# Second graph-attention layer: the projection h in twenty 128-column pieces, copied one pair later, and each head's sums normalised one pair earlier

## What is computed

```python
def gat_conv(x, src, dst, W, att_src, att_dst, bias, heads, out_ch):
    h = (x @ W).reshape(N, heads, out_ch)
    a_src = jnp.einsum('nhc,hc->nh', h, att_src)
    a_dst = jnp.einsum('nhc,hc->nh', h, att_dst)
    e = jax.nn.leaky_relu(a_src[src] + a_dst[dst], NEG_SLOPE)
    m = jax.ops.segment_max(e, dst, num_segments=N)
    ex = jnp.exp(e - m[dst])
    s = jax.ops.segment_sum(ex, dst, num_segments=N)
    alpha = ex / (s[dst] + 1e-16)
    out = jax.ops.segment_sum(h[src] * alpha[:, :, None], dst, num_segments=N)
    return out.reshape(N, heads * out_ch) + bias
```

## Time and profile before

| | us |
|---|---|
| median of three runs | 1220.93 |
| lowest and highest run | 1220.03 and 1222.17 |
| the profiled execution, its span | 1220.4 |
| in it: the 64 pairs of this layer, first sum to last `columns` | 909.4 to 1127.2 |

### The profile page before, as it was taken

The page is one execution under the profiler, slowest core; times in us unless marked ns, Lnnn a source line. Parts: engine busy times, 40 slices in busy tenths (PEclk is TensorE's granted clock), DMA queues, the critical chain, the costliest instruction groups (busy, mean ns, idle before and its releaser), DMA issues. The chain is left out here.

```text
span 1220.4 us, 17917 instructions
## 1 busy us (share of the span) xinstructions
PE 1052.0 (86%) x5617; PEld 744.6 (61%) x5622; DVE 778.0 (64%) x1724; ACT 524.2 (43%) x752; POOL 625.3 (51%) x503
## 2 busy tenths in 40 slices
PE   3999899989599999999298799888898888777897
PEld 1454577778477777777055488787773434433575
DVE  6988578628233333332495889996368777787855
ACT  2234544231111111111133478889537776766323
POOL 1000458302557555543410587999478777685242
PEclk9999899855599999999589799999989999989899
DMA  3000003044388999992510111211012111172551
GB/s 117 1 0 1 1 1 137 2 170 151 132 285 296 301 302 307 303 306 94 182 35 1 37 45 43 87 53 36 9 39 69 36 53 35 37 242 72 179 173 42
DMA packets 107987, 134.57 MB, mean 110 GB/s; under 512 B 30240, under 2 KB 76040, under 8 KB 107792
## 3 DMA queue, kind: packets, MB, share of 16 engines
q1 hardware_dynamic: 92720, 112.68, 28.4%
q0 software_dynamic: 15200, 21.04, 5.3%
HBM read 135.03 MB, written 27.45 MB: 133 GB/s over the span
## 5 line engine op out<-in xcount | busy, mean ns | idle before, releaser
L2347 POOL TENSOR_TENSOR am<-CT,qb 128x1024 f32<-128x1024 f32 x128 | 302.2, 2385 | 29.5 <-ACT PT L2376 17.4
L2369 ACT ACTIVATE PS<-adb,ab 128x1024 f32<-128x1024 f32 x128 | 143.1, 1118 | 89.4 <-DVE am L2474 88.2
L2474 DVE TENSOR_TENSOR am<-PS,am 128x1024 f32<-128x1024 f32 x128 | 156.4, 1222 | 37.3 <-ACT PS L2369 30.2
L2468 DVE CUSTOM_DVE_ANT_0 masked<-PS,mask 128x1024 f32<-128x1024 f32 x128 | 156.2, 1220 | 32.4 <-issue 30.6
L2580 PE MATMUL PS<-PT,h 128*65 128x512 f32 x256 | 122.8, 611 | 36.6 <-ACT PT L2376 25.1
L1232 DVE COPY yo<-PS 128x512 f32<-128x512 f32 x64 | 44.3, 691 | 168.5 <-PE PS L1170 163.1
L2567 PE MATMUL PS<-h,PT 128*128 128x129 f32 x1024 | 128.0, 283 | 22.0 <-ACT PT L2376 12.2
L2376 ACT ACTIVATE PT<-am,as 128x1024 f32<-128x1024 f32 x128 | 145.2, 1134 | 0.3 <-DVE am L2474 0.3
L2567 PEld LDWEIGHTS PS<-h,PT 128*128 128x128 f32 x1024 | 121.1, 196 | 30.5 <-issue 18.2
L1197 ACT ACTIVATE hT<-PS,b1T 128x128 f32<-128x128 f32 x128 | 40.0, 363 | 214.8 <-PE PS L1162 195.7
L1162 PE MATMUL PS<-xgT,w1r 128*128 128x128 f32 x1024 | 125.8, 276 | 0.0
(11 more groups left out here) (426 smaller groups left out, 1777.9 us busy)
## 6 DMA issues: line engine op xcount, KB each, us to landing
w2r<-in_L_ffn_W SPq DMA_DIRECT2D x64, 512.0 KB
w1r<-in_L_ffn_W SPq DMA_DIRECT2D x64, 512.0 KB
adb<-a_scratch SPq DMA_DIRECT2D x16, 512.0 KB, 4.0
qb<-q_scratch SPq DMA_DIRECT2D x14, 512.0 KB, 3.8
wc<-in_L_gnn_W SPq DMA_DIRECT2D x4, 1024.0 KB, 9.2
w1x<-in_L_ffn_W SPq DMA_DIRECT2D x2, 2048.0 KB, 11.0
w2x<-in_L_ffn_W SPq DMA_DIRECT2D x2, 2048.0 KB, 9.3
w1x<-in_L_ffn_W SPq DMA_DIRECT2D x7, 512.0 KB, 5.4
```

The source lines that it names most:

```text
L2347: pool.tensor_tensor(am[:, k % RING, :], CT[:, s, :], qb[:, hd % 2, :], ALU.add).then_inc(s_sum, 1)
L2369: act.activation(RELU, adb[:, hd % 2, :], ACT.Relu, bias=ab[:, s, hd:hd + 1]).then_inc(s_relu, 1)
L2468: dve.tensor_tensor_reduce(masked[:], wide(row_bank(hd)), mask[:, t, :], 1.0, -3.0e38, ALU.subtract, ALU.max, mrow[:, hd % 2, t:t + 1]).th ...
L2474: dve.tensor_tensor(am[:, k % RING, :], RELU, am[:, k % RING, :], ALU.add).then_inc(s_all, 1)
```

## The change

The ten units in the loop become twenty pieces of one tile by 128 columns: four for tiles 6 and 7 of heads 0 to 3, and sixteen for heads 4 to 7. `H_AT` puts them behind (0,1), (0,3), (0,5), (0,7), (1,4), (1,6), and in heads 2 to 5 behind s = 0, 4 and 6, in heads 3 and 4 behind s = 7 as well. ACT's copy comes LATE = 1 pair later. `normed` moves from behind the sum of the fifth pair (s = 4) to behind that of the fourth (s = 3). The counts for which `columns` and the weight load wait follow: SP issues the second half of W2 after 10 units, the last of which is now behind (0,7). The first attention layer keeps its numbers.

```diff
--- before.py
+++ after.py
@@ -2196,17 +2196,22 @@
             FQ = FH // 2
             quarters = [[(t + n, 1, slice(q * FQ, (q + 1) * FQ), slice(n * FQ, (n + 1) * FQ)) for n in range(2)]
                         for q in range(2) for t in range(0, NT, 2)]
+            UP_FRONT = 6
             if final:
-                UNITS = [[(t, 0, slice(0, FH), slice(0, FH))] for t in range(NT)] + quarters
-                H0 = 6
-                H_AT = (0, 1), (0, 3), (1, 1), (1, 5), (2, 1), (2, 5), (3, 5), (4, 1), (4, 5), (5, 1)
+                UNITS = [[(t, 0, slice(0, FH), slice(0, FH))] for t in range(UP_FRONT)]
+                for half, tiles in ((0, range(UP_FRONT, NT)), (1, range(NT))):
+                    UNITS += [[(t, half, slice(q * FQ, (q + 1) * FQ), slice(0, FQ))] for q in range(2) for t in tiles]
+                H0 = UP_FRONT
+                FIRST_HALF = UP_FRONT + 2 * (NT - UP_FRONT)
+                H_AT = ((0, 1), (0, 3), (0, 5), (0, 7), (1, 4), (1, 6),
+                        *((hd, s) for hd in range(2, 6) for s in (0, 4, 6, 7) if s < 7 or hd in (3, 4)))
             else:
                 UNITS = [[(NT - 1, 0, slice(0, FH), slice(0, FH))], [(NT - 1, 1, slice(0, FQ), slice(0, FQ))],
                          *([(t, 2, slice(0, FQ), out) for t, _, _, out in unit] for unit in quarters[NT // 2:])]
                 H0 = 3
                 H_AT = (0, 1), (0, 5), (1, 1)
             H_AFTER = dict(zip(H_AT, range(H0, len(UNITS))))
-            LATE = 3 if final else 2
+            LATE = 1 if final else 2
             H_MOVED = {(hd + (s + LATE) // NT, (s + LATE) % NT): i for (hd, s), i in H_AFTER.items()}
             assert H0 + len(H_AT) == len(UNITS)
 
@@ -2217,8 +2222,8 @@
                         return 2 if s == NT - 1 else 0
                     return 2 + s // 2 + 1
                 if hd < HEADS // 2:
-                    return s + 1
-                return NT + (hd - HEADS // 2) // 2 * (NT // 2) + s // 2 + 1
+                    return s + 1 if s < UP_FRONT else UP_FRONT + hd // 2 * (NT - UP_FRONT) + s - UP_FRONT + 1
+                return FIRST_HALF + (hd - HEADS // 2) // 2 * NT + s + 1
 
 
 
@@ -2289,7 +2294,7 @@
                             sp.dma_start(W2t[0][:], W2_d[:, :, 0:HEADS * CH2 // 2]).then_inc(s_w2[0], 16)
                         if final and hd == 1:
 
-                            sp.wait_ge(s_h, NT)
+                            sp.wait_ge(s_h, FIRST_HALF)
                             sp.dma_start(W2t[1][:], W2_d[:, :, HEADS * CH2 // 2:]).then_inc(s_w2[1], 16)
                         if final and hd == HEADS - 2:
                             tail.load_early(sp, len(UNITS))
@@ -2507,7 +2512,7 @@
                     for k in range(PAIRS):
                         hd, s = k // NT, k % NT
                         counted(k)
-                        if hd and s == (4 if final else 1):
+                        if hd and s == (3 if final else 1):
                             normed(hd - 1)
                         for ahead, t in maxima(hd, s):
                             maxed(ahead, t)
@@ -2645,7 +2650,7 @@
                         if (hd, s) in H_AFTER:
                             wait(pe, s_hm, H_AFTER[hd, s])
                             if final:
-                                if H_AFTER[hd, s] == NT:
+                                if H_AFTER[hd, s] == FIRST_HALF:
                                     pe.wait_ge(s_w2[1], 16)
                                 wait(pe, s_ev, hd if s > 2 else hd - 1)
                             else:
```

## The result

| | before | after |
|---|---|---|
| median, us | 1220.48 (4 runs) | 1236.07 (4 runs) |
| lowest to highest | 1219.96 to 1222.17 | 1234.18 to 1237.68 |
| span of the profiled execution | 1220.4 | 1235.8 |
| first sum of the loop to its last `columns` | 217.8 | 236.6 |

The changed kernel is slower by a factor of 1.012 (95% interval 1.0097 to 1.0144), 15.6 us between the medians, where 17.3 were forecast.

The account below looks back on a forecast made before the run. DVE and ACT were taken to set the pace, PE mattering only where one waits for it. +0.4 - 8.7 - 12.5 + 16.3 + 14.8 + 1.6 + 5.4 = +17.3 gave 1238.2 us on the median, range 1230.5 to 1244.0.

Parts of the forecast that it names:

- The waits that go: DVE's late maximum behind (hd,7), heads 1 to 4, -8.7 us; its wait for transposes, heads 1, 2, 4 and 5, -12.5.
- The normalising: Slot behind (hd,3), heads 1 to 5: DVE waits 2.41 us for transposes, slot 5.74 instead of 2.48; +16.3 us.
- The copies: With LATE = 1 ACT waits 1.46 us for a piece, making the next ReLU 1.2 late; +14.8 us together.
- One sign: A sign to look for in the profile: slots of 3.7 us behind s = 7 and about 3.7 behind s = 1.
- The clock: PE idle 3.84 us behind (hd,3) lowers its clock; columns of (hd,4) 1.34 longer in four heads of five, +5.4 us.
- after 3.06 us: Idle stretch of PE in the profile before, after which columns took 1.90 us as always.
- The rival that the clock holds: No fall of PE's clock after the new idle stretch: 1238.2 - 5.4 = 1232.8 us; chance 0.20.
- The one that it stays down over the next piece as well: Piece behind (hd,4) and next columns at half speed, head 2's offsets late: 5 x 3.1, +2, about 1250 us; chance 0.09.
- Heads 6 and 7: No pieces there; only the wait of the earlier normalising counts: +0.4 and +1.2, together +1.6 us.
- Off the path: Second half of W2 about 10 us later, head 2's offsets queue behind it: cost 0, bound 3 us.
- That PE is ahead of the copies: Faster rival: pieces ready when ACT comes, so the copies' +14.8 us go: 1218.0 us; chance 0.05.
- That the delays overlap: No-difference rival: a late ReLU before (hd,3) is taken up by DVE's wait for the transposes; 1222 us; chance 0.04.

Follow-up runs that it names:

- both_back: Changed kernel with LATE = 2 and the normalising behind s = 4 again, only the pieces and their places kept: 1209.47 us, 0.9870 of the kernel before.
- both_w2_later: both_back with SP issuing the second half of W2 behind the write of head 2's offsets: 1199.35 us, 0.9829 of the kernel before.
- norm_after_max: Changed kernel with the normalising still in the slot of (hd,3), but behind that slot's maximum: 1233.11 us, 1.0112 of the kernel before.
- norm_back: Changed kernel with only the normalising put back behind s = 4; pieces and LATE = 1 stay: 1219.45 us, 0.9953 of the kernel before.
- late_two: Changed kernel with LATE = 2, the normalising staying behind s = 3: 1227.19 us, 1.0018 of the kernel before.
- second profile of the change: The changed kernel run again, unaltered, on another chip: 1241.02 us, 1.0177 of the kernel before.
- the two tests with zeros: Changed kernel with ten matmuls of zeros behind columns of (hd,3), heads 1 to 5, run twice: 1234.48 us (1.0074 of the kernel before) and 1231.87 us (1.0093).
- last experiment: both_w2_later with eight maxima of head 7 moved from behind s = 0 and 1 to behind s = 5 and 6: 1199.75 us, 0.9824 of the kernel before.
- pe_kept_busy: Changed kernel with ten matmuls of zeros on PE behind columns of (hd,3) in heads 1 to 5, first run: 1234.48 us, 1.0074 of the kernel before.
- units_behind_six: Kernel before, with its four big units behind (hd,5) of heads 1 to 4 put behind (hd,6): 1220.86 us, 0.9993 of the kernel before.

## Why the prediction came out right, point by point

**The waits that go.** The slots behind (hd,7) of heads 1 to 4 are 2.54, which is 2.11 less than before where 2.17 were counted, and no maximum waits there. In the slots behind (hd,4), 2.47, the wait of 3.1 is gone. That the two are real gains, and not hidden by something else, is shown by both_back and both_w2_later: with the pieces alone the kernel gains 1.3% and 1.7%, 15.5 and 20.7 us, where 21.2 were taken off. Of the 5.7 that the first lacks, the late offsets are 3.4.

**The normalising.** 5.74 was worked out, and five slots of 5.74 or 5.75 were measured. That the wait is for the transposes was shown by norm_after_max, and that it costs 16.3 and more by norm_back.

**The copies.** Worked out were 1.46 us of waiting, 0.13 in which the copy holds ACT and a ReLU 1.2 late; the rows show 1.3 to 1.4 in most places where the clock held, 0.16, and slots of 3.68 and 3.65 (2.48 + 1.2). The late_two kernel takes nine tenths of the pieces' waiting away. One sign was put a pair too early: these slots stand behind s = 0 and 2 and not behind s = 7 and 1, as the ReLU behind a copy is that of the third pair on. The sum does not depend on it. Over heads 1 to 5 the slots grew by 13.7 where 13.6 were counted. In the whole LATE = 1 against LATE = 2 is 0.9953 against 0.9870 with the normalising late, 10 us, and 1.012 to 1.018 against 1.0018 with it early, 13 to 19 us. The term was 14.8. In these totals the copies are not alone: the clock and heads 0, 6 and 7 differ too.

**The clock.** This term came out by luck: a fall was costed too low and one fall too many was counted. I had 1.34 us in four heads; the profile has 1.6 to 1.7 in three, 5.0 instead of 5.4. The row from which the 1.34 came had the clock low for part of `columns` only: it took 3.24, and it takes 3.5 to 3.6 here. The second profile of the change has four, 8.7 us together, and the two tests with zeros put the clock at 5.0 us (heads 1 to 5 of one pair of profiles) and 9.2 (medians side by side). The forecast also read "after 3.06 us" as a length at which the clock holds; it does so in nine of twelve profiles and falls in three. The rival that the clock holds is out for this kernel. The one that it stays down over the next piece as well came true in two heads of the second profile, with slots 2.5 and 2.9 above 2.66, and the median of that chip, 1.0177 of before, is beyond the interval of the first: on 1220.93 it would be 1242.5, still in the range. The place where the clock's fall costs is also as foreseen: `columns` of (hd,4) itself has time to spare, and what is late is the piece behind it, then its copy, and so the slot behind (hd,6), 4.3 instead of 2.66.

**Sum of heads 0 to 5.** From the sum of (0,0) to that of (6,0) the forecast was 0.4 - 8.7 - 12.5 + 16.3 + 13.6 + 5.4 = 14.5, since the last copy counts in head 6. Measured: 174.15 - 159.20 = 14.95. Term by term: 0.6 for head 0, 8.4 and 12.6 taken off, 16.3 for the normalising, 13.7 for the copies, 5.0 for the clock, and 0.3 in the slot behind (5,7).

**Heads 6 and 7** were mis-sized. With the copy of (5,6) the forecast was 1.2 + 1.6 = 2.8 and they grew by 2.5 + 1.4 = 3.9. The clock fell there in both profiles: `columns` of (6,4), (6,5) and (7,0) took 2.44, 3.65 and 3.24 before, and those of (6,4), (6,7) and (7,0) took 3.6 after. And the other work of DVE in these heads meets POOL (last experiment). The two together took 58.6 us before, 62.5 after, 61.4 in norm_back, 61.2 in both_back and 58.5 in both_w2_later. Besides the copy's 1.2, two causes were seen at work; how much of the rest is whose stays open.

**Off the path.** The load of W2 came later, POOL waited 6.8 us for its offsets of head 2 and was in time, since its result was ready ahead of the sum at 966.6: the value 0 was right. But the margin belonged to the slow head 1. In norm_back and both_back, where that head is 3 us shorter, the same queue costs 1.7 and 3.4 us. I had named the cost with the bound 3 and had not seen that it hangs on the rest of the change.

**The rivals on the other side.** That PE is ahead of the copies was refused by 19 waits of ACT ahead of pieces. That the delays overlap was refused by 5.74 and 3.68 standing side by side in one head.

That 15.6 was measured where 17.3 was forecast is partly luck, as errors cancel. The loop is 18.8 longer instead of 17.3, and 3.4 us came back before and behind it, of which no term spoke and of which 1.2 are the clock. The range was not worked out either: its terms give 1231.2 with the clock holding and heads 6 and 7 at -1.6, and the rival of the longer low clock some 1250, neither of which is its end. The second set of runs, 1242.5 by its ratio, is 1.5 below the upper end.

## What to carry to other kernels

A copy that the critical engine makes of another engine's work needs a distance counted on both engines, from the earliest start of the producer to the place in the consumer's queue. One step instead of two turned some 0.15 us of work into 1.2 us of delay, eleven times by the sum's count. Smaller pieces are worth having, but they must not be bought with less slack: the same pieces with two steps of distance and the normalising where its input is ready were 1.3% faster than before instead of 1.2% slower, and 1.7% with the load of W2 moved as well. And a DMA that is in time behind a slow stretch is to be costed again as soon as that stretch becomes faster.

## What the runs showed of the hardware

**At this idle time the clock falls in some executions and not in others.** Five equal stretches of 3.83 or 3.84 us without matmuls per execution: the clock fell in three of them in one profile and in four in another, not the same ones. With 2.67 us idle (norm_after_max) it still fell in four of five, by slots of 4.1 to 4.4 behind (hd,6). Ahead of `columns` of (0,1) PE is idle for 3.06 us in all twelve profiles, and the clock fell in three of them (late_two, pe_kept_busy, units_behind_six; 3.64 to 3.65 us instead of 1.90). So between 2.67 and 3.84 us the length of the idle stretch alone does not tell whether the clock falls. With 1.67 or 1.68 us left behind the zeros it fell in none of ten. The Trainium skill ("TensorE: Matmul & The Clock Gate", Part 1) has the throttled clock as the default state that activity releases. That matmuls of zeros hold it at 2.4 GHz agrees. By the reading of the prediction all five stretches would have fallen, and that is not so.

**A short operation of DVE waits for a whole one of POOL.** An operation on 128 x 128 that reads two tiles in SBUF took 0.28 us alone and 2.42 beside POOL's addition of 2.36. Moving the eight of them away from POOL made all short, and two on 128 x 256 that then met it took 2.60 and 2.54 instead of 0.42. The sums of DVE, which read one operand from PSUM, took 1.21 to 1.23 with POOL working beside them and without. The Trainium skill ("SBUF — State Buffer", Who interferes with whom) tells of one pair of ports that DVE and GpSimd share and that one of them locks at a time, and names DVE instructions with two SBUF inputs as those that contend with a GpSimd instruction reading SBUF. The numbers agree with it.

**A scattered write is slow.** The offsets of a head go to memory in one DMA, and SP could issue their reading 8.7 to 13.9 us after it in both_w2_later, where no load of W2 is issued just ahead of any of them. For head 2 it was 13.7, 12.2 and 11.9 us in the three kernels both_back, norm_back and after, with the load of half of W2 issued 1.1 us ahead of the write, and 10.5 in both_w2_later with the load behind it. That the load ahead is what costs these 1.4 to 3.3 us is likely and not shown: the last head's write took 13.9 us without it.
